# Second attention of a two-layer block: low planes of the experts' weights on POOL, its head with ACT's and DVE's planes and half stores

## What is computed

```python
h = _layernorm(x, ln1_g, ln1_b)                       # x: 8 x 512 x 256
q, k, v = h @ Wq, h @ Wk, h @ Wv                      # 16 heads of 16 channels
scores = einsum('bhqd,bhkd->bhqk', q, k) / sqrt(16)
ctx = einsum('bhqk,bhkd->bqhd', softmax(scores), v)
x = x + ctx @ Wo
xt = _layernorm(x, ln2_g, ln2_b)
probs = softmax(xt @ Wg)                              # 8 experts, 2 of them per row
ye = gelu(xt @ W1 + b1) @ W2 + b2                     # W1: 8 x 256 x 1024, W2: 8 x 1024 x 256
```

## Time and profile before

| | |
|---|---|
| median of 3 runs | 2214.91 us |
| profiled execution, its own time | 2219.42 us |
| its span (first to last instruction) | 2217.5 us |
| granted TensorE clock, mean | 0.917 |
| PE matmul busy | 1799.8 us (81%) |
| DVE busy | 1569.2 us (71%) |
| ACT busy | 1385.3 us (62%) |
| POOL busy | 584.2 us (26%) |

### The profile page before, as it was taken

The page is one execution under the profiler, slowest core; times in us unless marked ns, Lnnn a source line. Parts: engine busy times, 40 slices in busy tenths (PEclk is TensorE's granted clock), DMA queues, the critical chain, the costliest instruction groups (busy, mean ns, idle before and its releaser), DMA issues. The chain is left out here.

```text
span 2217.5 us, 38421 instructions
## 1 busy us (share of the span) xinstructions
PE 1799.8 (81%) x12161; PEld 1093.2 (49%) x12162; DVE 1569.2 (71%) x3459; ACT 1385.3 (62%) x2644; POOL 584.2 (26%) x617
## 2 busy tenths in 40 slices
PE   4588888888888887867899998798883699999990
PEld 2355555555555554533234333333233588888870
DVE  3599899999899998756766667666736555555547
ACT  1398889898889899933666666666661233333333
POOL 5232324242424241131111221211111233333320
PEclk9699999899999999988999999998995799999995
DMA  1221212121212121012111134434346411111116
GB/s 53 67 77 39 78 36 80 37 80 37 79 37 79 37 69 46 25 40 61 35 49 35 58 99 131 144 120 129 120 134 257 171 47 47 47 45 45 41 35 230
DMA packets 142985, 170.62 MB, mean 77 GB/s; under 512 B 27233, under 2 KB 123698, under 8 KB 140786
## 3 DMA queue, kind: packets, MB, share of 16 engines
q1 hardware_dynamic: 135010, 149.59, 21.9%
q0 software_dynamic: 6816, 18.62, 2.7%
q10 hardware_dynamic: 1008, 0.54, 0.1%
HBM read 104.55 MB, written 64.09 MB: 76 GB/s over the span
## 5 line engine op out<-in xcount | busy, mean ns | idle before, releaser
L1291 DVE TENSOR_REDUCE NM<-sP 128x1 f32<-128x512 f32 x512 | 332.5, 684 | 181.0 <-PE sP L1169 178.4
L1101 ACT ACTIVATE PT<-tP 128x512 f32<-128x512 f32 x512 | 286.5, 602 | 202.1 <-PE tP L1180 201.2
L475 ACT ACTIVATE YZ<-YZ,gsc 128x512 f32<-128x512 f32 (+3 forms) x512 | 294.3, 616 | 0.0
L1555 ACT ACTIVATE H<-hP,B1T 128x256 f32<-128x256 f32 (+1 forms) x312 | 121.3, 454 | 255.7 <-PE hP L1635 204.5
L459 ACT ACTIVATE XL<-mP 128x512 f32<-128x512 f32 (+1 forms) x384 | 219.8, 573 | 95.8 <-PE mP L551 64.4
L722 DVE CUSTOM_DVE_ANT_0 YZ<-SeP,YZ 128x512 f32<-128x512 f32 (+3 forms) x512 | 242.0, 485 | 45.3 <-PE SeP L541 27.8
L540 PE MATMUL SeP<-SMV,SST 128*128 128x512 f16 (+3 forms) x512 | 157.3, 318 | 116.1 <-DVE mn L722 114.5
L467 ACT ACTIVATE PTa<-tPa 128x512 f32<-128x512 f32 (+1 forms) x384 | 222.4, 579 | 17.1 <-PE tPa L572 14.8
L1169 PE MATMUL sP<-STK,STQ 112*128 112x512 f16 x512 | 206.3, 405 | 29.6 <-DVE NM L1291 19.4
L1180 PE MATMUL tP<-STQ,STK 114*128 114x512 f16 x512 | 200.4, 396 | 25.7 <-ACT PT L1101 25.3
L566 PE MATMUL tPa<-ident,YZ 128*128 128x128 f32 x1280 | 217.3, 287 | 4.4 <-ACT PTa L467 3.6
(11 more groups left out here) (325 smaller groups left out, 3850.5 us busy)
## 6 DMA issues: line engine op xcount, KB each, us to landing
X<-in_L_ffn_W SPq DMA_DIRECT2D x32, 512.0 KB, 4.2
weight_planes<-X SPq DMA_DIRECT2D x64, 256.0 KB, 2.4
SST<-planes_a_scratch SPq DMA_DIRECT2D x384, 32.0 KB, 1.8
SMV<-planes_a_scratch SPq DMA_DIRECT2D x384, 32.0 KB, 1.8
planes_a_scratch<-HI SPq DMA_DIRECT2D x64, 128.0 KB, 1.7
planes_a_scratch<-LO SPq DMA_DIRECT2D x64, 128.0 KB, 1.8
Y<-results_scratch SPq DMA_DIRECT2D x16, 512.0 KB, 8.8
STQ<-planes_scratch SPq DMA_DIRECT2D x96, 64.0 KB, 2.6
```

What stands on the lines that cost most here:

```text
L475: act.activation(w, w, ACT.Square, scale=gsc[:, b % 2, i, hh:hh + 1]).then_inc(hyp_ready, 1)
L1101: act.activation(PT[:, p % 4, par, kt, :], tP[x % 3][:, :], ACT.Exp).then_inc(exp_done, 1)
L1291: dve.tensor_reduce(NM[:, g % 2, col:col + 1], sP[n % 2][:, :], AX.X, ALU.max, negate=True).then_inc(max_done, 1)
```

## The change

1. In the pieces, WLO moves from DVE to POOL, as two instructions: a scaling of WST in place by 128, and a subtraction of WHI. ACT's WHI is not changed.
2. For the first batch's q and k, ACT casts PSUM straight to HI, and DVE computes LO straight from PSUM; POOL has no part in it. The bank is free when DVE is done.
3. The four blocks of every batch come in the order 0, 2, 1, 3. For the first batch SP stores planes 0 and 2 first (pl_first), planes 1 and 3 afterwards (pl_stored). Half 0 waits for the first store alone.
4. Of the 12 loads of half 0, SP issues six and ACT the other six.
5. The memset of STK's last 32 rows is done in float32 words (3072 in place of 6144 elements).
6. For the second batch each q or k block of PE is split: its first matmul stays at its place, the second comes two tiles later.

```diff
+            SHIFT_PAIR = struct.unpack("<f", struct.pack("<ee", SHIFT, SHIFT))[0]
...
-            USES = [("h", 0, -11, 0), ("h", 1, -11, 4), ("q", 0, -8, 1), ("q", 1, -8, 5), ("q", 2, -7, 1), ("q", 3, -7, 5),
+            USES = [("h", 0, -11, 0), ("h", 1, -11, 4), ("q", 0, -8, 1), ("q", 2, -8, 5), ("q", 1, -7, 1), ("q", 3, -7, 5),
...
+            QORDER = [0, 2, 1, 3]
...
+                        if n == slot(-7, 0):
+                            sp.wait_ge(blo, 2)
+                            sp.dma_start(planes_d[0, 0, 0:2 * CH:2].rearrange("u p t -> p u t"), HI[:, 0:2 * CH:2, :]).then_inc(pl_first, 16)
+                            sp.dma_start(planes_d[0, 1, 0:2 * CH:2].rearrange("u p t -> p u t"), LO[:, 0:2 * CH:2, :]).then_inc(pl_first, 16)
+                        if n == slot(-6, 0):
+                            sp.wait_ge(blo, 4)
+                            sp.dma_start(planes_d[0, 0, 1:2 * CH:2].rearrange("u p t -> p u t"), HI[:, 1:2 * CH:2, :]).then_inc(pl_stored, 16)
+                            sp.dma_start(planes_d[0, 1, 1:2 * CH:2].rearrange("u p t -> p u t"), LO[:, 1:2 * CH:2, :]).then_inc(pl_stored, 16)
...
-                            sp.wait_ge(pl_stored, 32 * b + 32)
+                                sp.wait_ge(pl_first, 32)
+                            else:
+                                sp.wait_ge(pl_stored, 32 * b + 32)
...
-                            for par in range(2):
-                                for jj, planes in [(0, (0, 0)), (1, (0, 1)), (2, (1, 0))]:
...
+                            for par in range(2 if k > 0 else 1):
+                                for dst, q, key in staging(k, par):
...
+                        k = at_piece(n, 7)
+                        if k is not None:
+                            pool.wait_ge(w_high, k + 1)
+                            pool.tensor_scalar(WST, WST, SCALE, 0.0, ALU.mult, ALU.add).then_inc(w_scaled, 1)
+                            pool.wait_ge(w_scaled, k + 1)
+                            pool.tensor_tensor(WLO, WST, WHI, ALU.subtract).then_inc(w_low, 1)
...
+                        if n == slot(-3, 1):
+                            act.wait_ge(stg_set, 4)
+                            act.wait_ge(pl_first, 32)
+                            for dst, q, key in staging(0, 1):
+                                act.dma_start(STQ[dst:dst + D, 0, 1, :, :], q).then_inc(staged[0], 16)
+                                act.dma_start(STK[dst:dst + D, 0, :, :], key).then_inc(staged[0], 16)
...
-                                if b >= 1:
-                                    act.wait_ge(blo, 4 * (b - 1) + i + 1)
+                                if b == 0:
+                                    act.activation(HI[:, i, :], src[:, :], ACT.Copy,
+                                                   scale=float(D) ** -0.5 if i < CH else 1.0).then_inc(bhi, 1)
+                                    continue
+                                act.wait_ge(blo, 4 * (b - 1) + QORDER.index(i) + 1)
...
+                            if kind == "q" and at_batch(n - 2, step, t) == 1:
+                                pe.matmul(bank[nth["q", i, 1] % 2][:, :], WQ[:, 1, i * P:(i + 1) * P], hT[:, 1, 1, :],
+                                          start=False, stop=True).then_inc(bank_full, 1)
...
+                                if b == 1:
+                                    pe.matmul(dst[:, :], WQ[:, 0, i * P:(i + 1) * P], hT[:, b % 2, 0, :], start=True, stop=False)
+                                    continue
...
-                            dve.memset(STK[96:128, :, :, :], SHIFT).then_inc(stg_set, 1)
-                        k = at_piece(n, 7)
-                        if k is not None:
-                            dve.wait_ge(w_high, k + 1)
-                            dve.scalar_tensor_tensor(WLO, WST, SCALE, WHI, ALU.mult, ALU.subtract).then_inc(w_low, 1)
+                            dve.memset(STK[96:128, :, :, :].rearrange("p g q t -> p (g q t)").bitcast(F32), SHIFT_PAIR).then_inc(stg_set, 1)
+                        for j, u in enumerate(QORDER):
+                            if n == slot(-8 + j // 2, 3 + 4 * (j % 2)):
+                                dve.wait_ge(bhi, j + 1)
+                                dve.scalar_tensor_tensor(LO[:, u, :], bank[nth["q", u, 0] % 2][:, :], float(D) ** -0.5 if u < CH else 1.0,
+                                                         HI[:, u, :], ALU.mult, ALU.subtract).then_inc(blo, 1)
+                                dve.wait_ge(blo, j + 1)
+                                dve.engine_nop().then_inc(bank_out, 1)
```

More of the change, by code:

```diff
@@ L959, in piece_of, with staging @@
                 return a["L0_ffn_W2"][e].rearrange("(k p) c -> p k c", p=P)[:, rows * half:rows * (half + 1), :], 2, at
-            USES = [("h", 0, -11, 0), ("h", 1, -11, 4), ("q", 0, -8, 1), ("q", 1, -8, 5), ("q", 2, -7, 1), ("q", 3, -7, 5),
+            def staging(k, par):
+                views = []
+                for jj, planes in [(0, (0, 0)), (1, (0, 1)), (2, (1, 0))]:
+                    q, key = [planes_d[k // 2 % 2, planes[qk], CH * qk + k % 2].rearrange("(hh r d) t -> r d hh t", r=2, d=D)[par]
+                              for qk in range(2)]
+                    views.append((64 * par + D * jj, q, key))
+                return views
+            USES = [("h", 0, -11, 0), ("h", 1, -11, 4), ("q", 0, -8, 1), ("q", 2, -8, 5), ("q", 1, -7, 1), ("q", 3, -7, 5),
                     ("v", 0, -2, 0), ("v", 1, -2, 4), ("y", 0, 18, 2), ("y", 1, 18, 6), ("w", 0, 19, 4), ("w", 1, 20, 0),
                     ("m", 0, 23, 0), ("m", 1, 23, 4), ("l", 0, 24, 7)]
+            QORDER = [0, 2, 1, 3]
             nth = {}
@@ L1009, in _ @@
                                              shift_d[g % 2, :, TP * par:TP * par + TP, :].rearrange("r (q i) t -> r q (i t)", q=2)).then_inc(shifted[g % 2], 16)
+                        if n == slot(-7, 0):
[6 more added lines that the diff above has]
+                            sp.dma_start(planes_d[0, 1, 1:2 * CH:2].rearrange("u p t -> p u t"), LO[:, 1:2 * CH:2, :]).then_inc(pl_stored, 16)
                         b = at_batch(n, -6, 0)
-                        if b is not None:
+                        if b is not None and b >= 1:
                             if b >= 2:
@@ L1022, in _ @@
                                 sp.wait_ge(stg_set, 4)
-                            sp.wait_ge(pl_stored, 32 * b + 32)
+                                sp.wait_ge(pl_first, 32)
+                            else:
+                                sp.wait_ge(pl_stored, 32 * b + 32)
                             if k >= RING:
                                 sp.wait_ge(t_full, HALF * TP * (k - RING + 1))
-                            for par in range(2):
-                                for jj, planes in [(0, (0, 0)), (1, (0, 1)), (2, (1, 0))]:
-                                    dst = 64 * par + D * jj
-                                    q, key = [planes_d[b % 2, planes[qk], CH * qk + k % 2].rearrange("(hh r d) t -> r d hh t", r=2, d=D)[par]
-                                              for qk in range(2)]
+                            for par in range(2 if k > 0 else 1):
+                                for dst, q, key in staging(k, par):
                                     sp.dma_start(STQ[dst:dst + D, k % RING, par, :, :], q).then_inc(staged[k % RING], 16)
@@ L1057, in _ @@
                                 pool.memset(STQ[:, :, :, :, :].rearrange("p g r q t -> p (g r q t)").bitcast(F32), 0.0).then_inc(stg_set, 1)
-                        for u in range(2 * CH):
-                            b = at_batch(n, -8 + u // 2, 4 + 3 * (u % 2))
-                            if b is not None:
-                                if u == 0 and b >= 1:
+                        for j, u in enumerate(QORDER):
+                            b = at_batch(n, -8 + j // 2, 4 + 3 * (j % 2))
+                            if b is not None and b >= 1:
+                                if j == 0:
+                                    if b == 1:
+                                        pool.wait_ge(pl_first, 32)
                                     pool.wait_ge(pl_stored, 32 * b)
@@ L1125, in _ @@
                                     act.wait_ge(b_loaded, 144)
+                                if b == 1 and i == 0:
+                                    act.wait_ge(bank_out, nth["q", 3, 0] + 1)
                                 act.activation(hT[:, b % 2, i, :], src[:, :], ACT.Identity, scale=gcol[:, 0, i:i + 1],
```

7 lines of the change are left out of this document (6 added, 1 removed).

## The result

The changed kernel takes 2229.0 us (median of 5 runs, 2223.73 to 2229.33); the kernel before, on the same chip, 2214.87 us (5 runs, 2209.11 to 2215.45). The ratio on record is 1.0074, 95% interval 1.0056 to 1.0092, that of these two medians 1.0064: **0.6 to 0.7% slower**, where 2211.4 us was forecast. The profiled execution took 2229.15 us (span 2227.4); the one of before took 2219.42.

What follows compares the result with a forecast made beforehand. PE was taken to bound the tiles, with the pieces' cost seen as PE waiting. Terms -4.7 - 4.1 - 1 + 6.3 = -3.5 us gave 2215.9 us profiled, 2211.4 us as median; range 2203 to 2223.

Steps and rivals of the forecast that it cites:

- Terms 1 and 2: Head: earlier stores and loads start tile 0 sooner, -4.7 us; split blocks shorten tiles 0 to 16, -4.1 us.
- Term 3: POOL's pair for WLO: scaling 1.05 us and subtraction 2.2 us, 3.3 us together, bounds 3.2 to 4.4.
- The rival that made POOL's pair the bound: Pieces: at 4.4 us a pair, every piece has ACT waiting, giving 2222 us; chance 0.17.
- Term 4: Tiles with pieces: DVE's relief, a longer ring and held DVE instructions sum to -1 us, bounds -8 to +12.
- (b): Tiles with pieces: the ring through one buffer gets longer, costing where loads lack slack; +3 us, bounds 0 to +10.
- (c): Tiles with pieces: NMR on DVE is held by POOL through the shared port; +3 us, bounds 0 to +6.
- (a): Tiles with pieces: DVE, rid of WLO, makes PE wait less for maxima; -7 us, bounds -4 to -8.5.
- Term 5: Behind tile 511: nothing hides the longer ring, WHI to WHI 9.6 us against 7.5; +6.3 us, bounds +4 to +11.
- the three signs by which the forecast was to be seen as wrong: POOL's pair above 4 us, tile 0 staying at 1005 us, or ACT's waits for loads not growing.
- those for the pieces: Signs: maxima waits near 4 us, exponentials above 18, WHI to WHI 9.6, an NMR or rnb over 0.5 us.

Runs made afterwards that it cites:

- e1: The changed kernel with WLO back on DVE, so the new head alone: 2204.55 us, ratio 0.9954.
- e3: e1 with the second batch's q and k blocks whole again on PE: 2207.06 us, ratio 0.997.
- e9: The changed kernel with a second WST buffer and WLO back on DVE: 2190.47 us, ratio 0.9886.
- e6: e5 plus a POOL pair of the same size on a buffer of its own, for which nobody else waits: 2215.51 us, ratio 1.0005.
- e5: The changed kernel with WLO left out, high planes stored in its place, store and next load waiting for WHI alone: 2195.09 us, ratio 0.9916.
- e7: e5 plus two small round trips through DRAM by SP ahead of the stores: 2225.53 us, ratio 1.0049.
- e11: The changed kernel with a second WST buffer and WLO left out, high planes stored in its place: 2179.92 us, ratio 0.985.
- e10: e8 with POOL's pair cut into four scalings and four subtractions of 256 columns: 2191.33 us, ratio 0.9893.
- e8: The changed kernel with a second WST buffer, the next piece's load going out while one is worked on: 2204.66 us, ratio 0.9954.
- e4: e1 plus a POOL pair of the same size on a buffer of its own, for which nobody else waits: 2226.4 us, ratio 1.0061.

## Why the prediction was wrong

**Terms 1 and 2, right, sized a little low in the profile.** Forecast -8.8 us; the profiled stage gained 11.3 up to tile 32 (5.8 to tile 0, 5.5 behind it), each a little past its bound (-5.5 and -5). That e1's median came out at the same 8.8 is luck, its interval is 4 us to each side. The reasons held: PE runs from the values into tile 0 without idling, at the clock's upper level. Of the 5.5 us the split is worth 3.2; the other 2.3 were gained with whole blocks too (tile 0 to 32: 29.6 us before, 27.3 in e3, 24.1 in e1). A slip: 17.6 less 13.4 is 4.2, not 4.1.

**Term 3, right.** The pair was put at 1.05 and 2.2 us, and takes 1.05 and 2.13. The figures of the Trainium skill (GPSIMD Engine Reference, section Performance versus the Vector engine) by themselves don't give the 3.4 us that the prediction names: 1 and about 2.5 cycles for each of 1024 elements, at the 1.2 GHz that the same page states, make an estimate of 3.0 us, below the 3.2 measured. The sum doesn't use it. The rival that made POOL's pair the bound at 4.4 us came nearest (2222, 7 us short) for a reason that didn't occur.

**Term 4, the step that failed: the prices of (b), the longer ring, and (c), the held instructions.** Forecast -1 us with bounds of -8 and +12; measured +14.1 in the profile between tiles 264 and 511, and +24.4 for terms 4 and 5 together by medians (forecast +5.3).

(a), DVE relieved, was right: the waits for maxima fell by 7.2 us for the forecast 7.

(b), "It costs where the load has no slack ... four are so tight (3, 10, 16, 26)", +3 us. Two things failed. The delay itself was too small: "POOL, mostly idle, starts at once" held for 19 of pieces 0 to 26, but eight pairs began 0.7 to 5.6 us late, most of them behind planes or residual additions on POOL. The mean over all 27 is 0.9 us, about what DVE's WLO had. So WLO ended 1.9 us later behind WHI (2.3 to 4.2 us), not 1.1; up to the next load 1.5 us of it were left (4.3 to 5.8). The larger failure is the counting of slack piece by piece in the old timeline. A late load makes WHI late, which makes the next load late, and ACT stands with the exponentials queued behind the waiting WHI. Piece 10, with the change, where it had waited for nothing before:

```profile
1423.66 1.06 ACT L1123 ACTIVATE X<-X 128x1024 f16<-128x1024 f32 x1 [4.76 <-DMA X<-in_L_ffn_W]
```

Pieces 3, 10 and 16 waited 2.4, 4.8 and 2.8 us, forecast 1.0, 1.3 and 0.8, and 26 not at all; pieces 1, 15, 17, 21 and 22, which were not counted, waited 11.8 us more than before. In the whole stage 14 pieces waited for their load where 7 had, 46.5 us against 18.2. The largest stalls, pieces 4, 11 and 18, did stay (13.1 us before, 14.1 now). But they were no fixed sum: with two buffers no wait for a load is left, and the second buffer is worth 14.1 us with WLO on DVE (e1 less e9), so the ring already cost before the change.

(c), "four of the 17 NMR fall into it ... +3". The mechanism was right and its size wrong. Five NMR were held, each up to 2.24 us in place of 0.28, at pieces 6, 8, 13, 15 and 26; of the four pieces named only 8 came true. And five casts in front of NMR were held, which the prediction doesn't name; a cast has one input. Where nobody waits for the pair it costs 20.4 us (e6 less e5), with 16.2 us of NMR and casts held. DVE stands still in a hold, with the maxima behind it, and PE, which works in order, waits for NMR.

The two don't add up in general: a PE that waits for exponentials doesn't mind a late NMR. The pair on POOL is worth 24.7 us with two buffers, 20.4 beside a short ring, and only 3.5 separate the changed kernel from e7, which has a ring nearly as long and no holds. How much of the 24.4 us is "the ring's" therefore depends on which is taken away first, and stays open; that either alone is enough for a slowdown, of 21 us (e7 over e1) or of 11 (e6 over e1), doesn't. These two figures are low, as e6 and e7 have no WLO at all.

**A step that was missing.** Each term priced a wait of PE at its own length. The clock adds to it: of the 17.7 us between e1 and the changed kernel in the tiles with pieces 9.3 are slower matmuls. I had read the granted clock in the earlier trace rows (0.98 in both stretches) and used it for the head alone. It works on gains as on losses, so it would not have moved the sum of -1 much. As an estimate, at 0.7 us for each us of waiting (e11) the bounds of -8 and +12 become about -14 and +20, and these hold the 14.1; at the 0.2 of e7 they barely do.

**Term 5, right in its mechanism, its size in part luck.** WHI follows WHI by 9.4 to 10.1 us behind tile 511, forecast 9.6, ACT's timeline:

```profile
1641.97 1.06 ACT L1123 ACTIVATE X<-X 128x1024 f16<-128x1024 f32 x1
1652.03 1.06 ACT L1123 ACTIVATE X<-X 128x1024 f16<-128x1024 f32 x1 [3.63 <-DMA X<-in_L_ffn_W]
1661.48 1.06 ACT L1123 ACTIVATE X<-X 128x1024 f16<-128x1024 f32 x1 [3.78 <-DMA X<-in_L_ffn_W]
```

The stretch grew by 6.3 us against before, but only by 2.7 against e1, which has the ring of before: how much is left to do at tile 511 varies. From tile 264 to the routing before and e1 both take 390.8 us and the changed kernel 411.2, so terms 4 and 5 are best read as one, +20.4 in the profiles for the forecast +5.3.

The chances failed with it. The range ended at 2223, because (b) and (c) were bounded at +10 and +6 from a count on the old timeline. Either by itself measures more: 21 us for a ring 1.7 us longer than e1's (e7), and 20.4 us for the holds (e6 less e5).

None of the three signs by which the forecast was to be seen as wrong came up (tile 0 stood at 1004 us only because the whole stage began 4 us later), and those for the pieces all came true: maxima 3.9 us, exponentials 29.8, NMR above 0.5 us, WHI to WHI near 9.6. They told the direction of each wait and put no upper limit on one, so they couldn't tell a cost of +5 us from one of +20.

## What to carry to other kernels

Before work moves to a slower engine, ask what waits for the result and what shares a path with the engine: here a ring through one buffer grew by 1.5 us a round and POOL's long instructions were each able to stop DVE for all of their 2.1 us. Counted in the order of the table the first cost 10 us and the second 14 more than DVE's own work had. Slack counted round by round on the old timeline is no estimate where each late round starts the next one late, and a wait of TensorE costs more than its length where the granted clock moves with it (0.2 to 1.1 us more for each us here). A second buffer (24 us here with POOL, 14 with DVE) takes the ring away, and if POOL must work beside a busy DVE, short instructions do it: eight in place of two made POOL slower and the kernel 13 us faster, though no faster than leaving the work on DVE.

## What the runs showed of the hardware

- DVE's subtraction with two SBUF inputs is held until the POOL instruction that is running has ended: 2.24 us in place of 0.28, and rnb (L1318, at 1302.77 us) 1.83 in place of 0.16. In e10 NMR takes 0.66 us beside a subtraction of 256 columns. All 36 holds of the changed kernel, e8 and e10 end 0.07 to 0.14 us behind that POOL instruction, though POOL's next one often stands right behind it. The same cast that takes 0.21 us, from float32 in SBUF to float16 in SBUF, is held too (up to 2.01). The Trainium skill (GPSIMD Engine Reference, section Key points) names DVE instructions in a 2-port mode or with two SBUF inputs as contending with POOL. The trace agrees for the second kind; the cast would be of the first, but no run here shows its mode.
- Not held beside POOL: DVE's scaling of PSUM (nmf, 0.27 us from 1465.86 on, inside POOL's subtraction that held the next cast for 1.75), its product with one PSUM input (Yb, 423 to 425 ns over all 32, 24 of them beside POOL), and its statistics over SBUF, 0.42 us (16 beside POOL).
- A wait of PE costs more than its length: between kernels with the same 1362 matmuls, 24.3 us more of waiting came with 17.0 us more of matmul time, the granted clock at 0.91 in place of 0.97; other pairs of runs give 0.2 to 1.1 us for each us of waiting.
- POOL is held as well: in e4, beside DVE's WLO, its scaling took 1378 ns on the mean and 2075 at most, in place of 1047.
- POOL pays for short instructions: 256 columns take 405 ns for the scaling and 671 for the subtraction, where a quarter of the 1024-wide ones is 262 and 532.
